# One weight tensor and one transfer per unit of an expert layer, and six scatters instead of eight for its last chunk

## The chip, the cores and the metric

The kernel runs on one core of one Trainium2 chip. The metric is the device time of one execution in microseconds; the median of several runs is taken.

## The reference

The input is a batch of 32 images of 224 x 224. Each image becomes S = 1024 tokens of D = 64 numbers (patches of 7 x 7 times a matrix, plus a bias and a position). Two layers follow:

```
h = tok(x)                                # 32 x 1024 x 64
h = layernorm(h + attention(h))           # one head, softmax over 1024 keys
h = layernorm(h + ffn(h))

ffn: E = 8 experts, 256 hidden, top 1
  expert = argmax(softmax(h @ gate_w + gate_b)), prob = its probability
  the first CAP = 5120 tokens of each expert are kept, others give 0
  y = (relu(row @ w1[e] + b1[e]) @ w2[e] + b2[e]) * prob
```

All of it is in float32. What matters here is the expert layer: each of the 32768 tokens goes through the two matrices of its own expert, and the result goes back to the token's place.

## The kernel before, in words

**Two halves, interleaved.** A window b (the loop in `run_windows`, -2 to 33) works on attention for image b, prepares images b+1 to b+4, and finishes image b-1. Window b also scatters the 1024 rows of image b-2, each with its probability and token number (ROW = 66 numbers), from SBUF to a table in DRAM (`slots`), sorted by expert: GpSimd issues 8 indirect transfers of 128 rows (`scatter`, L1305). From the same table the expert layer reads units: 256 rows in a line (UNIT), all of one expert. Four units are a chunk, and there are NC = 34 chunks. VectorE works out from the counts per expert which units come next (`full_units` to `name_last`) and writes a table `tab` with a place and an expert for each.

**Where chunks run.** Chunks 0 to 26 run inside windows 6 to 32 (HOST), spread between the steps of attention. The remaining seven, 27 to 33, run after the last window, in `rounds`, where nothing else is left but the scatters. The last image's table (its chunks are 29 to 33, LAST = 29) names up to 20 units, for what is then left of every expert; a unit that has no rows is read from a dummy place whose token numbers are FAR, beyond the bounds check, so that its rows are written nowhere.

**One chunk.** SyncE's `load_chunk` (L407 to L431) waits for `table_ready`, reads four entries of `tab` into registers (L412), waits for the scatters of the images concerned and for the buffer to come free (NBUF = 5), and then issues, for each of the four units k with v = k // 2 and u = k % 2, three transfers: the rows to `b_in` (L427), the expert's w1 with b2 as a last column to `b_w1`, in the half of the partitions of u (L428), and its w2 with b1 as last columns to `b_w2`, on all partitions (L430). Each adds 16 to `c_loaded`, so TensorE and ScalarE wait for 96 per pair of units. The four units are two pairs v; in each, unit u = 0 sits on partitions 0 to 63 and u = 1 on 64 to 127 where rows are transposed.

Then: `rows_beside` (ScalarE L789) copies rows to `b_x`; `rows_turn` (TensorE L601) transposes them; `xT_copy` (ScalarE L796); `up` (TensorE L633, twice 4 products with w1); `rectify` (ScalarE L807, relu with b1); `down` (TensorE L649, 8 products with w2 that leave both units of a pair above each other); `sums_copy` (ScalarE L815 and L816) adds b2 and moves the sums to `b_yT`; `turn_back` (TensorE L610) transposes them back; on VectorE `weigh` (L1128), `finite` (L1135, L1136), `to_numbers` (L1141 to L1146), `residual_sum` (L1153 to L1158) and `centre` (L1162, L1166); `squares` (ScalarE L823), `sum_of_squares` (VectorE L1173), `deviation` (ScalarE L829), `scaled` (VectorE L1177, L1179) writes the finished rows `b_o`; and GpSimd's `spread_out` scatters them to the output with 8 indirect transfers of 128 rows (L1317). Tile j of the eight is u * 4 + v * 2 and 0 or 1, so tiles 6 and 7 are the unit k = 3.

**What sets the order.** Each engine has its list written out by hand. In `rounds` TensorE has, per chunk c: up(c, 0), turn_back(c-1), up(c, 1), rows_turn(c+1), down(c). VectorE has sum_of_squares(c-1), weigh(c), finite(c), scaled(c-1), and so on. GpSimd scatters chunks 25 to 33 one after the other after the last image's rows; before the first tile of chunk 29 (LAST) it waits until all scatters of earlier chunks have landed, as two of them may write one row. SyncE loads chunks 27 to 33 one after the other and then waits for the last scatters of each output buffer (L472).

In the windows, `sums_copy` reads the bank `p_misc`, and `qk_product` of a later image (TensorE L503) is the next to write there; it waits for `b_yT_ready`. From L503, `hi` and `lo` are made (ScalarE L744, VectorE L957) and copied by SyncE to `mQ`, `sK`, `mR` and `sR` (L444 to L461).

Of the kernel before, what the change touches and what calls it, by code (L numbers as in the profile page):

```python
# [18 lines left out]
D = 64  # L19
PATCH = 49  # L20
P = 128
# [61 lines left out]

def build(nc, x, posT, wqk, wide, deep, w1, w2, out):
    slots = nc.dram_tensor("slots", (SLOTS, ROW), F32, kind="Internal").ap()
    with ExitStack() as ctx:
# [107 lines left out]

        b_w1 = sb("b_w1", [P, NBUF, PAIRS, W1C])
        b_w2 = sb("b_w2", [P, NBUF, PAIRS, 2, W2C])
        b_in = sb("b_in", [P, NBUF, 2, CT, ROW])
# [188 lines left out]
        def _(sp):  # L386
# [20 lines left out]
            def load_chunk(c):  # L407
# [16 lines left out]
                for k in range(2 * PAIRS):  # L424
                    v, u = k // 2, k % 2
                    t = slice(v * UT, (v + 1) * UT)
                    sp.dma_start(b_in[:, r, u, t, :], unit_rows(at[k])).then_inc(c_loaded[r], 16)  # L427
                    sp.dma_start(b_w1[u * D:(u + 1) * D, r, v, :],  # L428
                                 w1[bass.ds(e[k], 1), :, :].rearrange("a k f -> (a k) f")).then_inc(c_loaded[r], 16)
                    sp.dma_start(b_w2[:, r, v, u, :], w2[bass.ds(e[k], 1), :, :].rearrange("a k f -> (a k) f"))\  # L430
                        .then_inc(c_loaded[r], 16)  # L431
# [39 lines left out]
            for r in range(NOUT):  # L471
                sp.wait_ge(b_scattered[r], 16 * NT * len(range(r, NC, NOUT)))  # L472


        @block.tensor
        def _(pe):
# [112 lines left out]
            def rows_turn(c):  # L589

                r = c % NBUF
                pe.wait_ge(c_loaded[r], 96 * PAIRS * (c // NBUF + 1))
                pe.wait_ge(b_x_ready, c + 1)
# [19 lines left out]
            def up(c, f):  # L613
# [16 lines left out]
                for v in range(PAIRS):  # L630
                    for u in range(2):
                        h = slice(u * D, (u + 1) * D)
                        pe.matmul(place[:, u, v * UNIT:(v + 1) * UNIT], b_w1[h, r, v, f * P:(f + 1) * P],  # L633
                                  b_xT[h, v, :], start=True, stop=True).then_inc(b_h_done, 1)

            def down(c):
# [9 lines left out]
                for v in range(PAIRS):  # L646
                    for f in range(HB):
                        for u in range(2):
                            last = pe.matmul(place[u * D:(u + 1) * D, v * UNIT:(v + 1) * UNIT],  # L649
                                             b_w2[:, r, v, u, f * D:(f + 1) * D], b_h[:, f, u, v, :],  # L650
                                             start=(f == 0), stop=(f == HB - 1))
# [77 lines left out]
        def _(act):  # L729
# [53 lines left out]
            def rows_beside(c):  # L783

                r = c % NBUF
                act.wait_ge(c_loaded[r], 96 * PAIRS * (c // NBUF + 1))
                if c >= 1:
# [11 lines left out]
            def rectify(c, f):  # L799
# [3 lines left out]
                for u in range(2):  # L803

                    act.wait_ge(b_h_done, 2 * PAIRS * (HB * c + f) + 2 * (PAIRS - 1) + u + 1)
                    for v in range(PAIRS):
                        act.activation(b_h[:, f, u, v, :], place[:, u, v * UNIT:(v + 1) * UNIT], ACT.Relu,  # L807
                                       bias=b_w2[:, r, v, u, HB * D + f:HB * D + f + 1]).then_inc(b_relu, 1)

            def sums_copy(c):  # L810
                r = c % NBUF
                act.wait_ge(b_y_done, c + 1)
                if c >= 1:
                    act.wait_ge(b_back_done, c)
                act.activation(b_yT[:, 0, :], banks(c)[2][:, 0:UNIT], ACT.Identity, bias=b_w1[:, r, 0, FF:W1C])  # L815
                act.activation(b_yT[:, 1, :], banks(c)[2][:, UNIT:2 * UNIT], ACT.Identity,  # L816
                               bias=b_w1[:, r, 1, FF:W1C]).then_inc(b_yT_ready, 1)

# [439 lines left out]
        def _(pool):  # L1258
# [89 lines left out]
            def rounds():  # L1348
                for c in range(INSIDE - 2, NC):
                    spread_out(c)  # L1350
            run_windows(step, rounds)

_INS = ["x", "posT", "wqk", "wide", "deep", "w1", "w2"]

# [58 lines left out]
```

## Time and profile before

| | |
|---|---|
| three runs | 1132.54, 1133.03, 1133.87 us |
| median | 1133.03 us |
| the profiled execution | 1133.07 us |
| its span, first to last instruction | 1131.2 us |
| TensorE busy (share of the span) | 1017.4 us (90%) |
| VectorE busy | 895.8 us (79%) |
| ScalarE busy | 690.0 us (61%) |
| GpSimd busy | 694.4 us (61%) |
| SyncE's transfers of weights | 136 of 65.0 KB and 136 of 64.2 KB |
| mean granted clock of TensorE | 0.949 of full speed |

Engines in the rows below: PE is TensorE's products, PEld its weight loads, DVE VectorE, ACT ScalarE, POOL GpSimd, SPq SyncE's queue. In a row of the timeline the first number is the start in microseconds from the span's start, the second the duration; then engine, line, operation, output<-input, partitions x elements, and in brackets the idle time before it and what ended it. TensorE's durations are modelled, and GpSimd's are rough.

### The profile page before, as it was taken

The page shows a single profiled execution, that of the slowest core. Times are in us where ns is not written, and L with a number is a line of the kernel's source. Part 1 is how long each engine was busy: PE and PEld are TensorE (multiplying, and loading weights), DVE is VectorE, ACT ScalarE, POOL GpSimd, SP SyncE. Part 2 cuts the span into 40 slices and gives each one's busy share as a digit, 9 for nine tenths or more (in the row PEclk, how much of TensorE's full clock was granted, in tenths as well). Part 3 has the DMA queues.
Part 4 walks back from the last instruction along what each step waited for, and adds up shares of the span by engine and source line. Part 5 has one row for each costly group of instructions (what it writes and reads, how often), then busy time and mean ns, then how long its engine had stood idle before and what let it go on. Part 6 is the DMA issues. An engine that isn't in the chain of part 4 may idle for free.

```text
span 1131.2 us, 19202 instructions
## 1 busy us (share of the span) xinstructions
PE 1017.4 (90%) x5534; PEld 575.3 (51%) x5534; DVE 895.8 (79%) x1843; ACT 690.0 (61%) x1073; POOL 694.4 (61%) x696
## 2 busy tenths in 40 slices
PE   4899999999999999999999999999999999855630
PEld 2455555555555555555555555555555555433320
DVE  5667787789888888989898988889898979475770
ACT  2355545667777677776667777766776666644530
POOL 0014444446767676666677676766766767777775
PEclk8699999999999999999999999999999999956875
DMA  5424334443435353444434343535344432123300
GB/s 129 100 70 102 97 90 116 102 108 93 117 100 131 87 135 99 118 114 102 103 104 117 92 119 97 135 87 134 99 117 109 99 76 62 34 67 94 100 29 8
DMA packets 87679, 110.01 MB, mean 97 GB/s; under 512 B 18892, under 2 KB 63903, under 8 KB 87574
## 3 DMA queue, kind: packets, MB, share of 16 engines
q1 hardware_dynamic: 70678, 91.67, 34.0%
q0 software_dynamic: 16896, 17.12, 4.7%
q8 instruction: 45, 0.74, 0.3%
q14 instruction: 60, 0.49, 0.1%
HBM read 40.69 MB, written 18.17 MB: 52 GB/s over the span
## 4 chain that ended last, share of the span: by engine, by line
PE 58%; DVE 25%; issue 6%; SPq 4%; POOL 2%; ACT 2%; DMA 2%; POOLq 0%; DVEq 0%; ACTq 0%
PE p_u L570 16%; PE p_st L554 9%; DVE mx L964 9%; PE p_st L557 7%; PE p_sm L540 6%; PE p_misc L503 4%; PE p_misc L526 4%; PE p_misc L585 3%; PE p_misc L633 3%; PE p_misc L649 2%; DVE ld L1015 2%; POOL out L1317 2%; SPq L428 1%; ACT xh L749 1%; SPq L427 1%
## 5 line engine op out<-in xcount | busy, mean ns | idle before, releaser
L1305 POOL DMA_INDIRECT slots<-rows,idx x256 | 261.4, 1021 | 216.7 <-issue 147.3
L964 DVE TENSOR_REDUCE mx<-p_sm 128x1 f32<-128x1024 f32 x252 | 307.3, 1220 | 78.9 <-PE p_sm L540 78.5
L766 ACT ACTIVATE pT<-p_st 128x1024 f32<-128x1024 f32 x256 | 262.2, 1024 | 162.5 <-PE p_st L557 158.9
L1317 POOL DMA_INDIRECT out<-b_o,b_ix x272 | 284.4, 1046 | 95.1 <-issue 73.3
L570 PE MATMUL p_u<-pT,vv 128*64 128x512 f32 x1024 | 262.9, 613 | 0.0
L554 PE MATMUL p_st<-mQ,sK 128*128 128x512 f32 x512 | 183.7, 440 | 5.3 <-ACT pT L766 3.4
L557 PE MATMUL p_st<-mR,sR 72*128 72x512 f32 x512 | 161.8, 397 | 0.0
L540 PE MATMUL p_sm<-sK,mQ 64*128 64x512 f32 x252 | 130.8, 519 | 7.1 <-DVE mx L964 3.4
L554 PEld LDWEIGHTS p_st<-mQ,sK 128*128 128x128 f32 x512 | 79.5, 189 | 103.6 <-issue 85.4
L540 PE MATMUL p_sm<-hi,mQ 64*128 64x512 f32 x252 | 130.6, 518 | 0.0
L557 PEld LDWEIGHTS p_st<-mR,sR 72*128 72x128 f32 x512 | 97.2, 190 | 22.6
L570 PEld LDWEIGHTS p_u<-pT,vv 128*64 128x64 f32 x1024 | 56.5, 135 | 96.2 <-issue 78.7
L807 ACT ACTIVATE b_h<-p_misc,b_w 128x256 f32<-128x256 f32 x244 | 95.5, 474 | 8.5 <-PE p_misc L633 3.9
L744 ACT ACTIVATE hi<-p_misc 128x1024 fp32r<-128x1024 f32 x32 | 32.8, 1024 | 100.7 <-PE p_misc L503 100.7
L540 PEld LDWEIGHTS p_sm<-sK,mQ 64*128 64x128 f32 x252 | 46.9, 186 | 87.4 <-issue 57.1
L1278 POOL TENSOR_TENSOR uc<-tt,hh 128x576 f32<-128x576 f32 x32 | 42.1, 1316 | 73.1 <-DVE tt L991 72.1
L526 PE MATMUL p_misc<-w_px,xt 114*128 114x137 f32 x504 | 76.6, 296 | 0.0
L633 PE MATMUL p_misc<-b_xT,b_w 64*128 64x256 f32 x488 | 73.3, 421 | 3.3 <-ACT b_h L807 1.7
L526 PEld LDWEIGHTS p_misc<-w_px,xt 114*128 114x128 f32 x504 | 63.7, 192 | 15.4 <-issue 15.4
L585 PEld LDWEIGHTS p_misc<-w_j,uu 128*128 128x128 f32 x512 | 62.0, 192 | 5.0 <-ACT uu L771 2.4
L585 PE MATMUL p_misc<-w_j,uu 128*128 128x73 f32 x512 | 61.1, 272 | 1.1 <-ACT uu L771 1.1
L633 PEld LDWEIGHTS p_misc<-b_xT,b_w 64*128 64x128 f32 x488 | 44.6, 197 | 30.3 <-issue 22.8
(191 smaller groups left out, 1508.0 us busy)
## 6 DMA issues: line engine op xcount, KB each, us to landing
mQ<-hi SPq DMA_DIRECT2D x64, 256.0 KB, 3.9
b_in<-slots SPq DMA_DIRECT2D x136, 66.0 KB
b_w<-in_w SPq DMA_DIRECT2D x136, 65.0 KB
b_w<-in_w SPq DMA_DIRECT2D x136, 64.2 KB
sK<-hi SPq DMA_DIRECT2D x32, 256.0 KB, 4.6
sK<-lo SPq DMA_DIRECT2D x32, 256.0 KB, 5.3
mR<-lo SPq DMA_DIRECT2D x32, 256.0 KB, 4.2
sR<-hi SPq DMA_DIRECT2D x32, 256.0 KB, 5.1
```

The source lines that it names most:

```text
L526: last = pe.matmul(projected(n, r)[:, j // 2, (j % 2) * GP:(j % 2 + 1) * GP], xt[0:KTOK, p, t * P:(t + 1) * P], w_px[:, :], start=True, st ...
L540: last = pe.matmul(max_place(n, j)[:, a, :], mQ[t][h, j * P:(j + 1) * P], keys[h, a * HALF:(a + 1) * HALF], start=True, stop=True)
L554: pe.matmul(p_st[:, a, :], sK[t][:, k * P:(k + 1) * P], mQ[t][:, a * HALF:(a + 1) * HALF], start=True, stop=False)
L557: last = pe.matmul(p_st[:, a, :], sR[p][0:D + NT, k * P:(k + 1) * P], mR[p][0:D + NT, a * HALF:(a + 1) * HALF], start=False, stop=True)
L570: last = pe.matmul(p_u[c:c + D, a, :], vv[:, p, k, :], pT[k % 4][:, a * HALF:(a + 1) * HALF], start=(r == 0), stop=(r == 3))
L585: last = pe.matmul(p_misc[:, j // 4, (j % 4) * GT:(j % 4 + 1) * GT], uu[:, j * P:(j + 1) * P], w_j[:, :], start=True, stop=True)
L633: pe.matmul(place[:, u, v * UNIT:(v + 1) * UNIT], b_w1[h, r, v, f * P:(f + 1) * P], b_xT[h, v, :], start=True, stop=True).then_inc(b_h_don ...
L766: act.activation(pT[k % 4][:, :], flat(p_st), ACT.Exp).then_inc(exp_done, 1)
L807: act.activation(b_h[:, f, u, v, :], place[:, u, v * UNIT:(v + 1) * UNIT], ACT.Relu, bias=b_w2[:, r, v, u, HB * D + f:HB * D + f + 1]).the ...
L964: dve.tensor_reduce(mx[:, p, j:j + 1], flat(max_place(n, j)), AX.X, ALU.max).then_inc(max_done, 1)
L1305: pool.indirect_dma_start(slots, bass.IndirectOffsetOnAxis(ap=idx[:, p, j:j + 1], axis=0), rows[:, p, j, :], None, bounds_check=SLOTS - 1, ...
L1317: pool.indirect_dma_start(out_rows, bass.IndirectOffsetOnAxis(ap=b_ix[:, o, j:j + 1], axis=0), b_o[:, o, j, :], None, bounds_check=T - 1, ...
```

## The change

On the host, w1 (with b2 as its column) is stored twice, one copy under the other, so that it has 128 rows, and beside it, in the same tensor, w2 and b1: `w` has 8 x 128 x 387 numbers. A unit's weights come in one transfer on all 128 partitions to `b_w`, at [v, u], so w1 lies on both halves of the partitions for either unit, and a half is read. A load has 8 transfers instead of 12 and the waits count 64 instead of 96. Since the column of b2 now lies at another place for u = 0 than for u = 1, `sums_copy` has four operations on 64 partitions and 256 columns instead of two on 128 partitions. For the last chunk `spread_out` leaves out tiles 6 and 7, and SyncE's last wait expects 32 less for its buffer.

```diff
--- before.py
+++ after.py
@@ -81,7 +81,7 @@
 DEEP = (KTOK, D, D, D, E, 1, KA)
 
 
-def build(nc, x, posT, wqk, wide, deep, w1, w2, out):
+def build(nc, x, posT, wqk, wide, deep, w, out):
     slots = nc.dram_tensor("slots", (SLOTS, ROW), F32, kind="Internal").ap()
     with ExitStack() as ctx:
         def sb(name, shape, dt=F32):
@@ -192,8 +192,7 @@
         t_rc = sb("t_rc", [P, LEFT])
         tab = sb("tab", [P, UNITS], U32)
 
-        b_w1 = sb("b_w1", [P, NBUF, PAIRS, W1C])
-        b_w2 = sb("b_w2", [P, NBUF, PAIRS, 2, W2C])
+        b_w = sb("b_w", [P, NBUF, PAIRS, 2, W1C + W2C])
         b_in = sb("b_in", [P, NBUF, 2, CT, ROW])
         b_x = sb("b_x", [P, CT, 2 * D])
         b_xT = sb("b_xT", [P, PAIRS, UNIT])
@@ -425,9 +424,8 @@
                     v, u = k // 2, k % 2
                     t = slice(v * UT, (v + 1) * UT)
                     sp.dma_start(b_in[:, r, u, t, :], unit_rows(at[k])).then_inc(c_loaded[r], 16)
-                    sp.dma_start(b_w1[u * D:(u + 1) * D, r, v, :],
-                                 w1[bass.ds(e[k], 1), :, :].rearrange("a k f -> (a k) f")).then_inc(c_loaded[r], 16)
-                    sp.dma_start(b_w2[:, r, v, u, :], w2[bass.ds(e[k], 1), :, :].rearrange("a k f -> (a k) f"))\
+
+                    sp.dma_start(b_w[:, r, v, u, :], w[bass.ds(e[k], 1), :, :].rearrange("a k f -> (a k) f"))\
                         .then_inc(c_loaded[r], 16)
 
             def step(b, c, third, has):
@@ -469,7 +467,8 @@
 
 
             for r in range(NOUT):
-                sp.wait_ge(b_scattered[r], 16 * NT * len(range(r, NC, NOUT)))
+                missing = 16 * UT if r == (NC - 1) % NOUT else 0
+                sp.wait_ge(b_scattered[r], 16 * NT * len(range(r, NC, NOUT)) - missing)
 
 
         @block.tensor
@@ -589,7 +588,7 @@
             def rows_turn(c):
 
                 r = c % NBUF
-                pe.wait_ge(c_loaded[r], 96 * PAIRS * (c // NBUF + 1))
+                pe.wait_ge(c_loaded[r], 64 * PAIRS * (c // NBUF + 1))
                 pe.wait_ge(b_x_ready, c + 1)
                 if c < INSIDE:
                     pe.wait_ge(t_ready, min(HOST[c], NB))
@@ -630,7 +629,7 @@
                 for v in range(PAIRS):
                     for u in range(2):
                         h = slice(u * D, (u + 1) * D)
-                        pe.matmul(place[:, u, v * UNIT:(v + 1) * UNIT], b_w1[h, r, v, f * P:(f + 1) * P],
+                        pe.matmul(place[:, u, v * UNIT:(v + 1) * UNIT], b_w[h, r, v, u, f * P:(f + 1) * P],
                                   b_xT[h, v, :], start=True, stop=True).then_inc(b_h_done, 1)
 
             def down(c):
@@ -647,7 +646,7 @@
                     for f in range(HB):
                         for u in range(2):
                             last = pe.matmul(place[u * D:(u + 1) * D, v * UNIT:(v + 1) * UNIT],
-                                             b_w2[:, r, v, u, f * D:(f + 1) * D], b_h[:, f, u, v, :],
+                                             b_w[:, r, v, u, W1C + f * D:W1C + (f + 1) * D], b_h[:, f, u, v, :],
                                              start=(f == 0), stop=(f == HB - 1))
                 last.then_inc(b_y_done, 1)
 
@@ -783,7 +782,7 @@
             def rows_beside(c):
 
                 r = c % NBUF
-                act.wait_ge(c_loaded[r], 96 * PAIRS * (c // NBUF + 1))
+                act.wait_ge(c_loaded[r], 64 * PAIRS * (c // NBUF + 1))
                 if c >= 1:
                     act.wait_ge(b_t_done, c)
                 act.activation(b_x[:, :, :].rearrange("p j (u d) -> p u j d", d=D), b_in[:, r, :, :, 0:D], ACT.Copy)\
@@ -805,16 +804,19 @@
                     act.wait_ge(b_h_done, 2 * PAIRS * (HB * c + f) + 2 * (PAIRS - 1) + u + 1)
                     for v in range(PAIRS):
                         act.activation(b_h[:, f, u, v, :], place[:, u, v * UNIT:(v + 1) * UNIT], ACT.Relu,
-                                       bias=b_w2[:, r, v, u, HB * D + f:HB * D + f + 1]).then_inc(b_relu, 1)
+                                       bias=b_w[:, r, v, u, W1C + HB * D + f:W1C + HB * D + f + 1]).then_inc(b_relu, 1)
 
             def sums_copy(c):
                 r = c % NBUF
                 act.wait_ge(b_y_done, c + 1)
                 if c >= 1:
                     act.wait_ge(b_back_done, c)
-                act.activation(b_yT[:, 0, :], banks(c)[2][:, 0:UNIT], ACT.Identity, bias=b_w1[:, r, 0, FF:W1C])
-                act.activation(b_yT[:, 1, :], banks(c)[2][:, UNIT:2 * UNIT], ACT.Identity,
-                               bias=b_w1[:, r, 1, FF:W1C]).then_inc(b_yT_ready, 1)
+                for v in range(PAIRS):
+                    for u in range(2):
+                        h = slice(u * D, (u + 1) * D)
+                        last = act.activation(b_yT[h, v, :], banks(c)[2][h, v * UNIT:(v + 1) * UNIT], ACT.Identity,
+                                              bias=b_w[h, r, v, u, FF:W1C])
+                last.then_inc(b_yT_ready, 1)
 
             def squares(c):
                 act.wait_ge(b_c_ready, c + 1)
@@ -1346,14 +1348,17 @@
                     scatter(b - 2, par, range(6, NT))
 
             def rounds():
-                for c in range(INSIDE - 2, NC):
+                for c in range(INSIDE - 2, NC - 1):
                     spread_out(c)
+
+
+                spread_out(NC - 1, range(NT - UT))
             run_windows(step, rounds)
 
 
 
 
-_INS = ["x", "posT", "wqk", "wide", "deep", "w1", "w2"]
+_INS = ["x", "posT", "wqk", "wide", "deep", "w"]
 
 
 def kernel(x, L0_tok_W, L0_tok_b, L0_tok_pos, L0_attn_Wq, L0_attn_bq, L0_attn_Wk, L0_attn_bk, L0_attn_Wv,
@@ -1387,8 +1392,7 @@
         "posT": columns(np.asarray(L0_tok_pos)[0].T),
         "wqk": np.concatenate([np.concatenate([wq.T, wk.T], axis=1),
                                np.concatenate([np.asarray(L0_attn_bq), np.asarray(L0_attn_bk)])[None]]),
-        "w1": up,
-        "w2": np.concatenate([down, bias1], axis=2),
+        "w": np.concatenate([np.concatenate([up, up], axis=1), down, bias1], axis=2),
         "wide": np.concatenate([
             np.eye(P, dtype=f), np.triu(np.ones((P, P), f), 1), sumcol,
             np.broadcast_to(np.arange(E, 0, -1, dtype=f), (P, E)),
```

## Rows read from the trace of the kernel before

**Rows 1.** The page: span, and the shares of the chain that ended last, by engine

```profile
span 1131.2 us, 19202 instructions
...
PE 58%; DVE 25%; issue 6%; SPq 4%; POOL 2%; ACT 2%; DMA 2%; POOLq 0%; DVEq 0%; ACTq 0%
```

**Rows 2.** Two windows; columns: stretch, length, busy PE, PEld, DVE, ACT, POOL, clock, DMA

```profile
861.90:923.20 61.30, 60.84 (x343) 34.56 (x344) 53.12 (x111) 42.28 (x65) 41.86 (x43) 1.00 0.42 103
```

**Rows 3.** The chain that ended last, from 990 us on, by line

```profile
by line: issue 24.0%; POOL out L1317 11.5%; SPq L428 10.0%; SPq L427 8.1%; SPq L430 7.8%; SPq L412 5.0%; POOL slots L1305 3.9%; DMA slots<-rows,idx 3.1%; DMA b_w<-in_w 2.7%; PE p_sm L649 2.6%; DVE b_o L1179 1.5%; DVE b_p L1128 1.5%; PE p_mi
```

**Rows 4.** SyncE's queue, load of chunk 29 and start of chunk 30's: start us, us

```profile
1026.90 0.34 SPq L427 DMA_DIRECT2D b_in<-slots  x1
1027.47 0.50 SPq L428 DMA_DIRECT2D b_w<-in_w  x1
1028.16 0.43 SPq L430 DMA_DIRECT2D b_w<-in_w  x1
1028.84 0.33 SPq L427 DMA_DIRECT2D b_in<-slots  x1
...
1033.87 0.45 SPq L430 DMA_DIRECT2D b_w<-in_w  x1
1036.92 0.34 SPq L427 DMA_DIRECT2D b_in<-slots  x1
```

**Rows 5.** The scatters of chunks 25 to 33: ns min/median/max, first and last start us

```profile
L1317 POOL DMA_INDIRECT out<-b_o,b_ix x72: 970/972/1490, 1025.7 to 1122.8; - x72
```

**Rows 6.** GpSimd in order of time: start, us, idle before it in brackets

```profile
1045.44 1.12 POOL L1317 DMA_INDIRECT out<-b_o,b_ix  x1 [0.30 <-issue]
1047.35 1.11 POOL L1317 DMA_INDIRECT out<-b_o,b_ix  x1 [0.79 <-DVE b_o L1179]
...
1068.09 1.49 POOL L1317 DMA_INDIRECT out<-b_o,b_ix  x1 [0.30 <-issue]
1071.85 0.97 POOL L1317 DMA_INDIRECT out<-b_o,b_ix  x1 [2.28 <-issue]
...
1113.84 0.97 POOL L1317 DMA_INDIRECT out<-b_o,b_ix  x1 [0.30 <-issue]
...
1122.77 0.97 POOL L1317 DMA_INDIRECT out<-b_o,b_ix  x1 [0.30 <-issue]
```

**Rows 7.** VectorE in order of time: b_o of chunks 27 and 33, one b_fin between

```profile
1045.86 0.69 DVE L1179 TENSOR_TENSOR b_o<-b_c,b_rs 128x512 f32<-128x512 f32 x1
...
1053.06 0.43 DVE L1135 TENSOR_SCALAR b_fin<-b_p 128x512 uint8<-128x512 f32 x1
...
1101.79 0.69 DVE L1179 TENSOR_TENSOR b_o<-b_c,b_rs 128x512 f32<-128x512 f32 x1
```

**Rows 8.** The end: GpSimd's drain and SyncE past its last wait (ns, start us)

```profile
L86 POOLq DRAIN  x1: 22557/22557/22557, 1108.5 to 1108.5; - x1
L86 SPq COMPARE_BRANCH  x1: 41/41/41, 1124.9 to 1124.9; - x1
```

**Rows 9.** Landing: one kind of issue (us from issue), one piece of the chain (start, us)

```profile
mQ<-hi SPq DMA_DIRECT2D x64, 256.0 KB, 3.9
...
1075.55 1.87 DMA b_w<-in_w
```

**Rows 10.** ScalarE waits for chunk 29's load

```profile
1035.88 0.63 ACT L789 ACTIVATE b_x<-b_in 128x512 f32<-128x512 f32 x1 [5.31 <-DMA b_w<-in_w]
```

**Rows 11.** A window, ScalarE and TensorE around the copy of the sums

```profile
802.53 0.47 ACT L815 ACTIVATE b_yT<-p_misc,b_w 128x256 f32<-128x256 f32 x1 [0.72 <-PE p_misc L649]
...
802.90 0.47 ACT L816 ACTIVATE b_yT<-p_misc,b_w 128x256 f32<-128x256 f32 x1
...
805.13 0.71 PE L503 MATMUL p_misc<-xh,w_qkh 114*128 114x512 f32 x2
```

**Rows 12.** ScalarE on 128 and on 50 partitions

```profile
806.81 1.02 ACT L744 ACTIVATE hi<-p_misc 128x1024 fp32r<-128x1024 f32 x1 [2.93 <-PE p_misc L503]
...
810.68 1.05 ACT L749 ACTIVATE xh<-xr 50x1024 fp32r<-50x1024 f32 x1
```

## The prediction

> **What bounds the kernel now.** The profiled execution took 1133.07 us, 1131.2 of it span and 1.87 around it; the median of the three runs, 1133.03, is 0.04 below it, so the sum is made against 1133.07 and moved by 0.04. I read the page first: the chain that ended last is TensorE for 58% and VectorE for 25% of the span, and SyncE's queue for only 4% [rows 1]. The reader is to ask where those 4% lie, since 136 of SyncE's transfers go away.
>
> Next, the windows view. In two windows of 61.3 us TensorE is busy for 60.84 and VectorE for 53.12, with the DMA engines at 0.42 [rows 2]. So in the windows, up to about 988 us, compute sets the time.
>
> Then the chain from 990 us on: SyncE's L427, L428, L430 and L412 stand in it with 31% together [rows 3]; of 142 us these are 44, or 3.9% of the span, so all of SyncE's 4% lie here and none in the windows. The timeline of its queue shows why. One unit costs 1.94 us of queue (1026.90 to 1028.84) and a chunk 10.02 (1026.90 to 1036.92), of which L428 takes 1028.16 - 1027.47 = 0.69 us per unit [rows 4]. A reader who stops here takes the rounds for bound by loads.
>
> GpSimd's view says otherwise. The 72 scatters of chunks 25 to 33 start between 1025.7 and 1122.8 us, median 0.97 us each [rows 5], and the last eight stand (1122.77 - 1113.84) / 7 = 1.276 us apart [rows 6]. 71 such steps are 90.6 us of the 97.1. The rest: 0.79 us of idle time instead of 0.30 before chunk 27, 2.28 instead of 0.30 before chunk 29 (the wait at LAST for all scatters before it), together 2.47, and about 4.0 by which scatters beside VectorE's work are longer than 0.97, up to 1.49 [rows 6]. Chunk 33's rows were ready at 1101.79 + 0.69 = 1102.48 [rows 7], yet its first scatter starts at 1113.84 [rows 6]: GpSimd is 11.4 us behind. It is the bound of the rounds, at 8 x 1.276 = 10.2 us a chunk, and SyncE's 10 us a chunk are hidden behind it. After the last scatter (1122.77 + 0.97 = 1123.74) SyncE passes its last wait at 1124.9, and GpSimd's drain, begun at 1108.5 us for 22.56, ends at 1131.06 [rows 8].
>
> **The change, part by part.**
>
> Two scatters go. They are the last to start on a saturated engine, nothing lies beside them, and nothing hides them: 2 x 1.276 = **-2.55 us**. The drain ended 7.3 us after the last scatter; I let it follow one for one. If it didn't follow at all, the end would stay; it is bounded by 0 and 2.55, and I take 2.55, since the drain is GpSimd's own. SyncE's final wait asks for 32 less on the semaphore of chunk 33, which are just these two.
>
> Four issues per chunk go, 136 in all. In the rounds a chunk's load gets 4 x 0.69 = 2.76 us shorter on the queue. Where does this matter for GpSimd? Only at its one wait for rows, before chunk 27: b_o of chunk 27 ended at 1045.86 + 0.69 = 1046.55 us [rows 7], and its scatter started 0.80 later [rows 6]. That b_o stands on VectorE behind weigh of chunk 28, which goes back to sums_copy and down of chunk 28, which stand on TensorE behind rows_turn of chunk 29, which waits for chunk 29's load. The load can't begin earlier (it waits for the last image's scatters, on GpSimd); its last issue would stand at 1033.87 - 2.76 = 1031.11. What is not shown is how long 198 KB take to land. The old b_w piece of 66 KB took 1.87 us, the 256 KB of mQ 3.9 [rows 9]; between them by size, 3.2, with 1.9 and 3.9 as ends. Now ScalarE starts on that chunk at 1035.88, 2.0 after the issue [rows 10]; then at 1031.11 + 3.2 = 34.3, 1.5 us earlier (0.9 to 2.9). The copy of the sums, below, gives back 0.74. Left are 0.8 us (0.1 to 2.1), and the wait is worth 0.79 - 0.30 = **-0.49 us** (0.1 to 0.49). From there on, GpSimd is the slower one again in each round, and the shorter loads are worth nothing.
>
> In the windows, the 2.76 us per window are worth nothing: SyncE is in no part of the chain there [rows 1, 3], and TensorE is busy all through [rows 2]. What stands behind the load in its queue (the patches, mR and sR) goes out 2.7 us earlier, and nobody waits for it. If TensorE's cover were gone, this would be a gain, not a cost.
>
> More bytes: w1 is loaded for both halves, 66 KB per unit more, 264 KB per window. At 0.42 of DMA share and 103 GB/s [rows 2] that is 264 KB in 30.65 us, 9 GB/s more, and the share goes to some 0.46. Cost 0, under TensorE's 60.84 of 61.3 us. In the rounds a unit brings 266 KB in 1.25 us of queue; if transfers were slower than that, they would still hide behind the 10.2 us of scatters. Bounds: -0.5 and +1.0 over the whole kernel.
>
> sums_copy becomes four operations of 64 partitions instead of two of 128. The two start 0.37 us apart and last 0.47 [rows 11]. For half the partitions no row shows the same operation; nearest is a copy of 1024 columns, 1.02 us on 128 partitions and 1.05 on 50 [rows 12], so I take 0.37 for each added one: +0.74 us per chunk, with 0 and 4 x 0.47 - 0.84 = 1.04 as ends. In a window the next to want p_misc is TensorE's qk_product: b_yT was ready at 802.90 + 0.47 = 803.37, and L503 started at 805.13 [rows 11], 1.76 us of slack, so nothing shows. In the rounds 0.74 lies on the way to b_o, counted above. For chunk 33 it delays b_o from 1102.48 against a need at 1113.84: nothing.
>
> VectorE against GpSimd: scatters beside VectorE's work take up to 1.49 us, those with none beside them 0.97 [rows 6], 4.0 us in all. VectorE's operations stay the same in number, and all still stand beside scatters, so I leave the 4.0 as it is (3.5 to 4.5). Here a rule bears. The Trainium skill (SBUF — State Buffer, "SBUF: two separate sides") has the port pair of VectorE and GpSimd as an exclusive lock, under which GpSimd can't write descriptors until the VectorE operation ends. The trace agrees that there is a cost, but 0.52 us at most is less than one whole b_o of 0.69. That rule as a full block is a rival below.
>
> Sum: 1133.07 - 2.55 - 0.49 = 1130.03, less the 0.04 to the median: **1130.0 us**, 0.27% faster.
>
> **The rivals.**
>
> The rounds are bound by loads (0.05). For it: the chain's 31%. The five loads from chunk 29 to 33 would each give 2.76, less 1.3 for the later landing at the end: -12.5, and with -2.55 and -0.04 this is 1118.0 us. Against it: 0.30 us of idle time before nearly each scatter, and the 11.4 us of backlog.
>
> The end doesn't follow, or the windows pay a little (0.23, both land at no change). If the drain gives back less than one for one, 1130.5 to 1132.5. If each of the 27 windows with a chunk pays 0.05 to 0.1 us for the added copies and bytes, +1.4 to +2.7: 1131.4 to 1132.7. For it: nothing but that TensorE has under 0.5 us of slack in 61.3 [rows 2]. Against it: 1.76 us of slack at the hand-over.
>
> VectorE shuts GpSimd out for longer (0.04, slower). Place: the rounds, where shorter loads draw VectorE's operations closer together. If b_fin, b_pos and b_neg (0.43 each) and b_o (0.69) [rows 7] each held a scatter back for their full length, seven rounds would cost 7 x 1.98 = 13.9 instead of 4.0: +9.9, and with the 3.0 of gain 1139.9 us. It decides once the stretching grows by 5.3 us (3.0 of gain and 2.3 of the 0.2%), from 0.57 to 1.3 us a round. Against it: the rounds already take 10 us with VectorE's seven inside, and never did. The Trainium skill's SBUF page, named above, states this full block, and by it the result would be this rival's.
>
> **How the numbers follow.** About 0.2%, 2.3 us, is what a measurement of this kernel can tell from no change. The forecast has 0.68; the load rival 0.05 is faster too, and the case of no change 0.23, slower 0.04. The forecast's own range, from its bounds: -0.1 on the second term to -0.49, ±1 for bytes and stretching, ±0.5 for the runs' spread: 1129.0 to 1131.4. To hold 8 in 10 I go up to 1131.9, into the second case, and leave out the load rival and the slower one. Of the forecast's 0.68 a part (0.02) falls above 1130.77, so faster 0.71, same 0.25, slower 0.04.
>
> **What would show it.** 70 scatters instead of 72 in the last stretch, still 1.276 apart at the end, with chunk 27's first after 0.30 of idle time and not 0.79; the last scatter's end about 1120.7; the drain's end 7.3 us behind it; SyncE's chunk in the rounds 7.3 us instead of 10.0 and the wait of rows_turn shorter, yet the backlog before chunk 33 grown beyond 11.4; windows still 61.3 us a pair; L503 not waiting for the copies. I am wrong if the pairs lengthen by 0.1 or more, if the 2.28 us before chunk 29 change, or if GpSimd waits for b_o in the later rounds.

## The result, and the profile after

The kernel after took 1129.37 us (median of 22 runs, 1126.3 to 1132.0) where the kernel before, run on the same chip in turns with it, took 1131.65 (22 runs). The ratio is 0.997, with an interval of 0.9961 to 0.9979: 3.4 us faster, 2.4 to 4.4; the two medians lie 2.28 us apart. The prediction was 3.04 us and 1130.0. The profiled execution took 1127.63 us, 5.4 less than the profiled one before. The predicted gain is thus near the measured one in these runs, below it in the second series further down (5.0 us, 3.4 to 6.6) and too small in the pair of traces, so the question is where these 5.4 us lie, and which of them belong to the change.

The page of after: span, chain by engine, and SyncE's queue q1 (packets, MB, share of the 16 engines).

```profile
span 1125.8 us, 18858 instructions
q1 hardware_dynamic: 59798, 100.61, 35.8%
PE 59%; DVE 25%; issue 7%; ACT 4%; POOL 3%; DMA 1%; SPq 1%; POOLq 0%; DVEq 0%; ACTq 0%
b_w<-in_w SPq DMA_DIRECT2D x136, 193.5 KB
```

SyncE's queue had 4% of the chain [rows 1] and now has 1%. That is some 34 us of the chain, and the kernel is not 34 us faster: the chain only runs another way through the rounds. From 990 us on, by line:

```profile
by line: issue 25.0%; PE p_sm L648 14.8%; POOL out L1319 12.2%; ACT b_h L806 11.0%; ACT b_yT L817 6.1%; POOL slots L1307 6.0%; ACT b_sq L825 2.8%; DVE b_vs L1175 2.6%; DMA b_w<-in_w 2.2%; DMA slots<-rows,idx 1.6%; ACT b_x L788 1.5%; SPq L42
```

Where SyncE's lines stood with 31% [rows 3], there are now TensorE's `down` (L648), ScalarE's `rectify` (L806) and the copies of the sums (L817). A chain follows one of several paths of nearly the same length; the share of a path is not what shortening it brings.

The stretch from the first window's product of `qk_product` to the one near 897 us holds most of the windows; then the window of [rows 2] (columns as there).

```profile
63.05:896.53 833.48, 827.21 (x4557) 466.74 (x4556) 715.09 (x1445) 583.62 (x883) 526.97 (x523) 1.00 0.45 114
861.90:923.20 61.30, 60.75 (x344) 34.53 (x342) 53.08 (x110) 44.46 (x71) 41.77 (x42) 1.00 0.43 110
```

And the same stretch before:

```profile
64.40:897.48 833.08, 826.97 (x4558) 466.62 (x4556) 715.33 (x1445) 558.45 (x837) 527.06 (x523) 1.00 0.43 106
```

ScalarE has 25.2 us more to do, and the DMA engines carry 114 GB/s instead of 106; the length goes from 833.08 to 833.48. SyncE's load of chunk 29 and the start of chunk 30's, as in [rows 4]:

```profile
1025.70 0.33 SPq L426 DMA_DIRECT2D b_in<-slots  x1
1026.25 0.33 SPq L428 DMA_DIRECT2D b_w<-in_w  x1
1026.84 0.33 SPq L426 DMA_DIRECT2D b_in<-slots  x1
...
1030.02 0.34 SPq L428 DMA_DIRECT2D b_w<-in_w  x1
...
1032.97 0.34 SPq L426 DMA_DIRECT2D b_in<-slots  x1
```

A unit costs 1.14 us (1.94 before), a chunk 7.27 (10.02). GpSimd in the rounds, all 70 scatters and then in order of time, as in [rows 5, 6]:

```profile
L1319 POOL DMA_INDIRECT out<-b_o,b_ix x70: 969/972/1488, 1024.5 to 1117.5; - x70
```

```profile
1046.00 1.05 POOL L1319 DMA_INDIRECT out<-b_o,b_ix  x1 [0.30 <-issue]
...
1065.64 1.20 POOL L1319 DMA_INDIRECT out<-b_o,b_ix  x1 [0.30 <-issue]
1068.85 0.97 POOL L1319 DMA_INDIRECT out<-b_o,b_ix  x1 [2.01 <-issue]
...
1111.12 0.97 POOL L1319 DMA_INDIRECT out<-b_o,b_ix  x1 [0.30 <-issue]
...
1117.50 0.97 POOL L1319 DMA_INDIRECT out<-b_o,b_ix  x1 [0.30 <-issue]
```

Chunk 27's first scatter (1046.00) no longer waits for its rows. The last ends at 1118.47, and the drain 7.1 us later (1106.8 + 18.74 = 1125.54), to be read beside [rows 8]:

```profile
L86 POOLq DRAIN  x1: 18743/18743/18743, 1106.8 to 1106.8; - x1
L86 SPq COMPARE_BRANCH  x1: 41/41/41, 1119.7 to 1119.7; - x1
```

Cut at four marks, the 5.40 us of span are these. "Stretching" is the sum over the scatters of what each took beyond 0.972 us.

| stage | before | after | difference |
|---|---|---|---|
| start to the product of the first window | 64.40 | 63.05 | -1.35 |
| from it to the product near 897 us | 833.08 | 833.48 | +0.40 |
| from there to chunk 25's first scatter | 128.23 | 127.97 | -0.26 |
| that scatter to the end of the last | 98.03 | 93.97 | -4.06 |
| of it: two scatters, 2 x 1.276 | | | -2.55 |
| of it: wait before chunk 27 | 0.79 | 0.30 | -0.49 |
| of it: wait before chunk 29 | 2.28 | 2.01 | -0.27 |
| of it: stretching | 3.90 | 3.12 | -0.78 |
| last scatter to the end | 7.46 | 7.33 | -0.13 |

### The profile page after: what moved, and what is told of

Its sections match the earlier page's. It is cut to its first block, busy times and chain, and to the rows that moved or that the text cites. A ratio compares the mean times of both kernels' runs of the same rounds, so it can differ in the third digit from the quotient of the medians.

```text
span 1125.8 us, 18858 instructions
## 1 busy us (share of the span) xinstructions
PE 1019.9 (91%) x5534; PEld 576.2 (51%) x5534; DVE 895.2 (80%) x1843; ACT 727.6 (65%) x1141; POOL 691.4 (61%) x694
## 3 DMA queue, kind: packets, MB, share of 16 engines
q1 hardware_dynamic: 59798, 100.61, 35.8%
## 4 chain that ended last, share of the span: by engine, by line
PE 59%; DVE 25%; issue 7%; ACT 4%; POOL 3%; DMA 1%; SPq 1%; POOLq 0%; DVEq 0%; ACTq 0%
PE p_u L569 16%; PE p_st L553 9%; DVE mx L966 9%; PE p_st L556 7%; PE p_sm L539 6%; PE p_misc L502 4%; PE p_misc L525 4%; PE p_misc L584 3%; PE p_misc L632 3%; PE p_misc L648 2%; PE p_sm L648 2%; POOL out L1319 2%; DVE ld L1017 2%; ACT b_h L806 1%; ACT xh L748 1%
## 5 line engine op out<-in xcount | busy, mean ns | idle before, releaser
L806 ACT ACTIVATE b_h<-p_misc,b_w 128x256 f32<-128x256 f32 x244 | 95.6, 475 | 8.2 <-PE p_misc L632 3.4
L525 PEld LDWEIGHTS p_misc<-w_px,xt 114*128 114x128 f32 x504 | 63.7, 192 | 15.5 <-issue 15.5
## 6 DMA issues: line engine op xcount, KB each, us to landing
b_w<-in_w SPq DMA_DIRECT2D x136, 193.5 KB
```

Source lines behind the costliest of these rows:

```text
L525: last = pe.matmul(projected(n, r)[:, j // 2, (j % 2) * GP:(j % 2 + 1) * GP], xt[0:KTOK, p, t * P:(t + 1) * P], w_px[:, :], start=True, st ...
```

## The experiments

Two figures are read from each profiled execution: the **rest**, the span less the start-up up to that first product (1066.80 us before, 1062.75 after), and the **tail**, from chunk 25's first scatter to the end of the last (98.03 and 93.97).

The diffs show the lines that make the experiment; the waits that count the same transfers or scatters were changed with them and are left out.

**What is the kernel's, and what the execution's?** The kernel after once more, unchanged (no diff).

> The kernel after, not altered: a second execution to see what is the kernel's and what is the execution's. Theory: from the first window's product near 64 us to the end it takes 1062.75 us again, within 0.3; what lies before that product, which no part of the change touches, comes out anywhere between 62.5 and 67 us. Rival (the 63.05 us of the first execution is of the change's making): 63.05 again, within 0.3, and the span 1125.8.

Measured: ratio 0.9956 [0.9942, 0.997], that is 5.0 us, where the first series gave 3.4. The product stands at 65.29 us, not at 63.05, the span is 1127.3, the rest 1062.01 and the tail 93.79.

```profile
65.29:898.22 832.93, 826.83 (x4557) 467.20 (x4556) 716.20 (x1445) 583.42 (x883) 526.71 (x523) 1.00 0.45 114
```

In eleven profiled executions of ten kernels that product lies anywhere from 62.56 to 67.12 us, and no edit touches what runs ahead of it. So the -1.35 is not the change's. The rest differs by 0.74 between two executions of one kernel, more than the 0.3 I had allowed, and most of that is the long stretch (833.48, 832.93); before (833.08) lies between them, so the +0.40 is no cost that can be shown. The tail repeats within 0.2, and it is the stage to compare.

**The two parts apart.** The kernel before with the scatters' edit alone, and the kernel after without it:

```diff
-                for c in range(INSIDE - 2, NC):
+                for c in range(INSIDE - 2, NC - 1):
                     spread_out(c)
+                spread_out(NC - 1, range(NT - UT))
```

> Theory A (GpSimd's 80 steps of 1.276 us set the end of the rounds): two scatters fewer alone give -2.55 us, the end follows one for one, GpSimd's drain ends 7.3 us after the last scatter. Idle time before chunk 27 (0.79 us) and before chunk 29 (2.28 us) stays. Rival B (the rounds are bound by SyncE's loads): 0 us. Rival C (the windows pay for the weights' part of the change): the windows here are those of before, and this version beats the whole change by what they pay.

> Theory A: the one wait before chunk 27 goes (-0.49 us), the wait at chunk 29 and the stretched scatters give some tenths (-1.0 us in the trace of the whole change), the windows pay up to +0.4 us: -0.5 to -1.5 us. Rival B (loads bound the rounds): -12 us. Rival C (the windows pay): 0 or slower.

Measured, scatters alone: ratio 0.9972 [0.9961, 0.9984], rest 1064.21 (-2.59), tail 95.65 (-2.38). Weights alone: 0.9982 [0.9968, 0.9995], rest 1065.24 (-1.56), tail 96.53 (-1.50). The two rests add up to -4.15, and both edits together gave -4.05. The weights' edit thus gives a little more than the 0.5 to 1.5 us expected of it. GpSimd before chunk 29, with the scatters' edit alone and with the weights' alone:

```profile
1070.00 1.49 POOL L1318 DMA_INDIRECT out<-b_o,b_ix  x1 [0.31 <-issue]
1074.01 0.97 POOL L1318 DMA_INDIRECT out<-b_o,b_ix  x1 [2.52 <-issue]
```

```profile
1064.94 1.21 POOL L1318 DMA_INDIRECT out<-b_o,b_ix  x1 [0.30 <-issue]
1068.17 0.97 POOL L1318 DMA_INDIRECT out<-b_o,b_ix  x1 [2.02 <-issue]
```

The wait at LAST goes with the scatter ahead of it. Where that scatter was stretched to 1.49 us the wait was 2.28 [rows 6] or 2.52; where it took 0.97 to 1.21, in eight other executions, it was 2.01 or 2.02 (in the eleventh, weights_in_four, GpSimd waits there for b_o). The 0.27 so comes from which scatter VectorE meets, and appears with the weights' edit. That edit also brings the stretching down: 2.84 us alone, against 3.90 before and 4.04 with the scatters' edit.

The wait before chunk 27 did not do what was expected of it. With the scatters' edit alone it is 0.56 us (0.79 was to stay), and with the weights' edit alone it is 0.60 and not gone:

```profile
1044.58 1.23 POOL L1318 DMA_INDIRECT out<-b_o,b_ix  x1 [0.60 <-issue]
```

Here b_o of chunk 27 ends 19.98 us after chunk 25's first scatter and the scatter starts at 20.77, 0.79 later, as before (20.84 and 21.64). GpSimd came to the wait earlier, because fewer of the scatters ahead of it were stretched. Wait and stretching ahead of it are one term: as long as b_o comes last, what one loses the other gains.

**The issues or the copies?** The kernel after, with w1's own half and w2 in transfers of their own again, so that a chunk has twelve issues and only the copies of the sums differ from before:

```diff
-                    sp.dma_start(b_w[:, r, v, u, :], w[bass.ds(e[k], 1), :, :]...
+                    sp.dma_start(b_w[h, r, v, u, 0:W1C], w[bass.ds(e[k], 1), h, 0:W1C]...
+                    sp.dma_start(b_w[:, r, v, u, W1C:W1C + W2C], w[bass.ds(e[k], 1), :, W1C:W1C + W2C]...
```

> The whole change, but w1 for its own half alone and w2 in a transfer of their own again: 12 issues per chunk and the bytes of before, with the four operations for the sums and the six scatters. Theory A: the shorter loads are worth at most 1.5 us of the whole change, so -1.5 to -2.6 us against before, with chunk 27 waiting again, by 1 us more than before, since the sums come 1.06 us later. Rival B: no gain beside before. If the windows' +0.4 us come from the bytes they are gone here; if from the four operations, they stay.

Measured: ratio 0.9984 [0.9972, 0.9996], tail 95.59, that is 1.62 over after.

```profile
1049.98 1.11 POOL L1323 DMA_INDIRECT out<-b_o,b_ix  x1 [2.21 <-DVE b_o L1185]
```

Chunk 27's first scatter waits 2.21 us, 1.91 more than after. Its b_o of chunk 27 ends at 21.80 us from chunk 25's first scatter, 1.88 later than after and 0.96 later than before. So at this one place the added copies cost about what they last, and the four issues taken away pay for them with room to spare; everywhere else twelve issues bring no wait. With twelve issues stretching (2.82) and the wait at LAST (2.02) are as low as after. The number of issues is not their cause. What this version shares with after and not with scatters_only is the four copies; that these move the rhythm of ScalarE and VectorE in the useful direction is argued from that, not tested by itself. Its long stretch takes 832.72 us, so neither bytes nor issues show there.

**How far are the loads from being the bound?** The kernel after, with the weights of chunks 27 to 33 in four transfers of 32 partitions:

```diff
+PARTS = [1 if c < INSIDE else 4 for c in range(NC)]
-                    sp.dma_start(b_w[:, r, v, u, :], w[bass.ds(e[k], 1), :, :]...
+                    for g in (slice(i * P // PARTS[c], (i + 1) * P // PARTS[c]) for i in range(PARTS[c])):
+                        sp.dma_start(b_w[g, r, v, u, :], w[bass.ds(e[k], 1), g, :]...
```

> The kernel after, with the weights of a unit in four transfers of 32 partitions for chunks 27 to 33, the bytes the same: 20 issues a chunk in place of 8. By undisturbed steps of 0.57 us an issue a chunk's load takes 11.4 us and some 2.5 between chunks, 14 in all, over the 10.3 to 11.0 us in which GpSimd issues a chunk's scatters. Theory (GpSimd bounds the rounds only as long as SyncE's load is shorter than it): chunk 33's load ends near 1096 instead of 1074, its rows follow some 23 us later and its last scatter 8 us after those, so the kernel ends 5 to 15 us later than after, 1134 to 1144. Rival (the loads are far enough ahead that the rounds still end by GpSimd's count): 1128 to 1131.

Measured: 1145.01 us, ratio to before 1.0113 [1.0086, 1.0139]; tail 109.49, 15.5 over after. SyncE, ScalarE and GpSimd, a row or two of each:

```profile
1054.67 0.36 SPq L429 DMA_DIRECT2D b_in<-slots  x1
...
1068.53 0.36 SPq L429 DMA_DIRECT2D b_in<-slots  x1
```

```profile
1053.46 0.63 ACT L792 ACTIVATE b_x<-b_in 128x512 f32<-128x512 f32 x1 [2.60 <-DMA b_w<-in_w]
```

```profile
1052.05 1.11 POOL L1323 DMA_INDIRECT out<-b_o,b_ix  x1 [1.88 <-DVE b_o L1185]
```

Now a load does last longer (13.9 us between these two starts) than a chunk of scatters, GpSimd waits for b_o ahead of each chunk from 26 to 31, and the tail follows: seven waits make 17.8 us, 14.0 more of idle time than after has, and stretching is 4.67 (+1.55). This is how a round bound by loads looks, and neither before nor after looks like it. The tail is half a microsecond beyond the 15 us that I had allowed, and the median about one beyond 1144. I had reckoned from chunk 33's load to its own rows; but TensorE turns the rows of chunk c + 1 ahead of `down` of chunk c, and VectorE makes b_o of chunk c - 1 behind `weigh` of c, so the load of chunk 33 holds back the rows of chunk 31, and three chunks of scatters follow it.

**Does the end follow?** The kernel after without any scatter of chunk 33 (its rows are not written):

```diff
-                spread_out(NC - 1, range(NT - UT))
```

> The whole change without the other six scatters of the last chunk (its rows are left out). Theory A: 6 x 1.276 = 7.66 us less than the whole change, about -11 us against before (0.990), the drain's end 7.3 us behind the last scatter; the backlog is then chunk 32's. Rival (the end doesn't follow GpSimd one for one, a floor by the drain): less than 6 us beyond the whole change.

Measured: ratio 0.9887 [0.987, 0.9904]; rest 1054.54, tail 85.89. Against the two executions of after the tail is 8.08 and 7.90 shorter; six steps of 1.276 are 7.66, the rest is stretching. The end comes 6.86 us behind the last scatter (7.33 after): it follows one for one and a little more.

**How much room has the hand-over of the sums?** In the windows of after the four copies last 1.90 us, and the next product in their bank starts 1.24 us behind their end (835.12 - 833.88), in the other kind of window 0.69 (804.03 - 803.34). Before it was 1.76 in that one [rows 11].

```profile
801.43 1.91 ACT L817 ACTIVATE b_yT<-p_misc,b_w 64x256 f32<-64x256 f32 x4 [0.72 <-PE p_misc L648]
...
804.03 0.71 PE L502 MATMUL p_misc<-xh,w_qkh 114*128 114x512 f32 x2
...
831.98 1.90 ACT L817 ACTIVATE b_yT<-p_misc,b_w 64x256 f32<-64x256 f32 x4
...
835.12 0.71 PE L502 MATMUL p_misc<-xh,w_qkh 114*128 114x512 f32 x2
```

To see whether that slack is the room there is, the copies of the windows are cut into eight operations of 128 columns, and into sixteen of 64:

```diff
+                        for part in (range(4) if c < INSIDE else (slice(0, UNIT),)):
+                            n = slice(part * D, part * D + D) if c < INSIDE else part
-                        last = act.activation(b_yT[h, v, :], ...
+                            last = act.activation(b_yT[h, v, n], ...
```

> The whole change with sums_copy in eight operations of 64 partitions x 128 columns in the windows (chunks 0 to 26), four in the rounds. Theory A (the hand-over of p_misc has slack, 0.69 us in one kind of window and 1.24 in the other, with the copies at 1.90 us): eight operations last about 8 x 0.37 = 3.0 us, so 1.1 us more, which shows as 0.4 us in 12 of 23 windows and not in the others: +5 us against the whole change, with TensorE's qk_product waiting for the sums there. Rival (ScalarE has more slack than the rows show, the chain takes another way): no change against the whole change. Rival (the slack was already gone with four): +1.1 us in each of 23 windows, +25 us.

Measured: ratio 0.9974 [0.9959, 0.9988], rest 1063.44, nothing to tell from after, where 5 us more were expected. I had the eight too long: they last 2.50 us and end 0.15 us before the product.

```profile
803.80 2.50 ACT L820 ACTIVATE b_yT<-p_misc,b_w 64x128 f32<-64x128 f32 x8 [0.72 <-PE p_misc L648]
...
806.45 0.70 PE L502 MATMUL p_misc<-xh,w_qkh 114*128 114x512 f32 x2
```

> The kernel after, with the sums of a window's chunk copied by sixteen operations of 64 x 64 instead of four of 64 x 256. Theory (the copies have a slack of their own at the hand-over to the image's products, 0.69 us in one kind of window and 1.24 in the other, and eight operations of 2.50 us in all used up all but 0.14 and 0.65 of it): the sixteen last about 4.0 us, 1.5 longer than the eight, so the hand-over is late by about 1.3 us in one kind and 0.9 in the other, and 22 windows are 15 to 30 us longer; the whole about 1145 to 1160. Rival (another releaser of the same operations hides it, so that the slack that I read is not the room there is): 1127 to 1133, as with eight.

Measured: 1148.6 us, ratio 1.0142 [1.0115, 1.017]; rest 1082.78, 19.3 over the eight.

```profile
788.99 3.67 ACT L820 ACTIVATE b_yT<-p_misc,b_w 64x64 f32<-64x64 f32 x16
...
792.80 0.71 PE L502 MATMUL p_misc<-xh,w_qkh 114*128 114x512 f32 x2 [0.69 <-ACT b_yT L820]
```

Now TensorE does wait for the copies: 23 times before L502, 18.3 us in all, where it did so in no window after. The sixteen are 1.17 us longer than the eight; less what those left over (0.15 and 0.65) that is 1.02 and 0.52 a window, some 18 us over 23 windows. So the slack read in the trace is the whole cover, with nothing else behind it, and the change spent 1.07 of its 1.76 us without a price.

**What stretches the scatters?** The kernel after without `finite` and `to_numbers` in chunks 27 to 33, that is without the replacing of numbers that are not finite: five VectorE operations a round less (the test for finite numbers, two clamps, their sum and the copy by the test). `residual_sum` reads b_p in place of b_n.

```diff
-                    finite(c)
+                    if c < INSIDE:
+                        finite(c)
-                    to_numbers(c)
+                    if c < INSIDE:
+                        to_numbers(c)
```

> The whole change without the replacement of numbers that are not finite in chunks 27 to 33 (b_fin, b_pos, b_neg, b_n are left out and b_p is added as it is): five of VectorE's operations less per round. Theory A (GpSimd bounds the rounds, VectorE touches the end only by stretching scatters beside it, 3.2 us in all): -1 to -2.5 us against the whole change, by shorter scatters and not by earlier rows. Rival (the stretching doesn't come from VectorE): 0. Rival (VectorE bounds the rounds): 7 x 2.5 = -17 us.

Measured: ratio 0.9977 [0.9966, 0.9988], rest 1060.78, tail 91.90. Stretching falls from 3.12 to 0.76 us, and the scatters longer than 1.0 us from 17 to 4.

```profile
L1327 POOL DMA_INDIRECT out<-b_o,b_ix x70: 969/972/1264, 1028.7 to 1119.6; - x70
```

The tail is 2.07 us shorter (stretching -2.36, a wait of 0.56 before chunk 28 +0.26). What VectorE does beside them is what lengthens the scatters. The ratio does not show these 2 us (it is no lower than after's), and this profiled execution had the longest start-up of all, 67.12 us.

The traces show how. Scatters of before [rows 6] and after, and VectorE beside them:

```profile
1068.03 0.73 DVE L1146 COPY_PREDICATED b_n<-b_fin,b_p 128x512 f32<-128x512 uint8 x1
```

```profile
1065.30 0.69 DVE L1181 TENSOR_TENSOR b_o<-b_c,b_rs 128x512 f32<-128x512 f32 x1
```

```profile
1044.73 0.97 POOL L1319 DMA_INDIRECT out<-b_o,b_ix  x1 [0.30 <-DVE b_o L1181]
1044.79 0.69 DVE L1146 TENSOR_TENSOR b_n<-b_pos,b_neg 128x512 f32<-128x512 f32 x1
```

The copy ran when the scatter of 1068.09 started, and ended at 1068.76; the scatter ended at 1069.58, 0.82 later. b_o ended at 1065.99; the scatter that had started within it, at 1065.64, ended at 1066.84, 0.85 later. b_n, which began after its scatter, cost that scatter nothing. In the rounds of the eleven executions 172 of 768 scatters started when an operation of these kinds or a TENSOR_SCALAR had begun over 0.03 us before and had over 0.13 us to run, and each ended 0.80 to 0.85 us after the operation did. Where the operation in progress was a TENSOR_REDUCE or b_p, which reads PSUM (142 scatters), 140 took 0.97, and of the other 454, with none or one just begun or nearly over, 453 took 0.97 or 0.98. So a scatter's stretching is what is left of one operation at the scatter's start, less the first 0.13 us.

## Where the prediction was right, and the step that failed

**The bound.** Right: GpSimd bounds the rounds, and SyncE's 10 us a chunk were hidden. The rival with loads as the bound asked for -12.5; the weights' edit alone gave -1.56, and of the loads tried only the one of 13.9 us a chunk shows loads as the bound.

**Two scatters, -2.55.** Right. Alone they gave -2.59 in the rest and -2.38 in the tail, and the end followed.

**Shorter loads, -0.49 before chunk 27.** Right in place and working, and in the size of the wait; its worth was counted too high. 193.5 KB landed 3.01 us after the last issue (3.2 taken): ScalarE starts at 1033.05, the issue at 1030.02. Counted from chunk 25's first scatter, b_o of chunk 27 ended at 19.92 us instead of 20.84, 0.9 earlier where 0.8 was predicted, and the wait went to 0.30. But chunk 27's first scatter itself started only 0.14 us earlier (21.50 instead of 21.64), since more of the scatters ahead of it were stretched; in the second execution of after it was 0.75 earlier (20.89), and with the weights' edit alone 0.60 us of wait stayed. The term should have been taken together with the stretching ahead of it.

```profile
1030.02 3.01 DMA b_w<-in_w
```

```profile
1033.05 0.63 ACT L788 ACTIVATE b_x<-b_in 128x512 f32<-128x512 f32 x1 [5.82 <-DMA b_w<-in_w]
```

**The copies, +0.74 in length and 0 in price.** The price was right, the length not: four copies of 64 partitions last 1.90 us, +1.06, just beyond my upper end of 1.04. Two on 128 partitions started 0.37 apart [rows 11]; the four start 0.48 apart, each after the end of the one before. Had the cover been under 1.06 instead of 1.76, the error would have cost 0.3 us in each of 23 windows for every 0.3 missing; that is an estimate from sums_in_sixteen, where 23 windows paid.

**More bytes, 0.** Right: the long stretch is 832.93 and 833.48 against 833.08, with q1 at 100.61 MB.

**The backlog before chunk 33, to grow beyond 11.4 us.** Wrong, without a price. It fell to 7.5:

```profile
1102.90 0.69 DVE L1181 TENSOR_TENSOR b_o<-b_c,b_rs 128x512 f32<-128x512 f32 x1
```

b_o of chunk 33 ends at 1103.59 and its first scatter starts at 1111.12. Counted from chunk 25's first scatter its rows are ready at 79.09 us (76.77 before; 78.90 in the second execution, 79.10 with the weights' edit alone), so with shorter loads they come later and not earlier. Two things lie on their way: 1.06 us more of copies in each round, and TensorE's clock, granted at 0.80 between 1025 and 1100 us before and at 0.73 after, both means of time at 2.4 and at 1.2 GHz (columns as in [rows 2]; before, then after):

```profile
1025.00:1100.00 75.00, 41.27 (x252) 24.27 (x248) 49.08 (x98) 34.93 (x87) 56.10 (x55) 0.80 0.29 76
```

```profile
1025.00:1100.00 75.00, 41.54 (x228) 23.34 (x224) 47.55 (x96) 40.41 (x95) 56.54 (x56) 0.73 0.34 94
```

No run tells the two apart. GpSimd is still behind by 7.5 us, which is why nothing was lost.

**VectorE and the scatters, 4.0 unchanged.** This step failed. After has 3.12 and 2.94 us, below my lower end of 3.5, and the wait at LAST, which I had put at no change without a reason though I named it among the signs of being wrong, gives 0.27 more. The two together are -1.05, and they make up the difference between the tail predicted (-3.04) and the one measured (-4.06). I had argued that as many operations stand beside scatters as before; but a scatter pays only for what is left of the operation in progress at its start, that is decided by tenths of a microsecond, and the whole rhythm had moved by nearly one. Over the ten executions that keep VectorE's operations the sum lies anywhere from 1.95 (sums_in_sixteen) to 4.67 us (weights_in_four). That it fell and did not rise was luck: no step of the change's working makes it smaller.

**The Trainium skill's rule** (SBUF — State Buffer, "SBUF: two separate sides"). The page has an exclusive lock between GpSimd and a VectorE operation in a two-port mode, or with two SBUF inputs if GpSimd's operation reads SBUF too: the one that starts first has the port pair for its whole instruction. The 172 scatters agree with it as far as GpSimd waits: each is held until the VectorE operation ahead of it ends, and neither TENSOR_REDUCE nor b_p holds one (the profile does not show an operation's mode). I had read both the rule and the trace wrongly. That 0.52 us, the longest stretching, is less than the 0.69 of a b_o says nothing against a full block, since the operation was already under way. And the rival's price, each operation at its full length, 13.9 us, is not what the rule makes of these rounds: from the operations in progress at the scatters' starts (end + 0.84 us) the sum is 3.27 us after and 4.14 before, and 3.12 and 3.90 were measured. The rival's +9.9 is out. The other half of the rule, VectorE held for a whole scatter, does not show: b_o and b_n took their 0.69 us inside a scatter, while b_fin, when it began 0.52 to 0.63 us into one, took 0.70 and 0.59 instead of 0.43.

**The number.** Against the first series the prediction is 0.4 us short of the middle of an interval of 2.4 to 4.4 us, and against the second 2.0 short (3.4 to 6.6). Against the one profiled execution it is 2.4 short: 1.0 of it the tail, 1.35 the start-up, and this second part no argument from the change could have given.

## What to carry to other kernels

A path's share of the chain is not its worth: ask for the engine that has a backlog, since only its own work and its own waits move the end. Before an operation on a covered path is lengthened, read the gap between its end and its reader's start; that gap was here the whole of the cover, down to 0.15 us. When a change shifts the rhythm of two engines that disturb each other, look in the timeline at what one was doing when the other started, give the disturbance a range from zero up and do not carry its sum over unchanged; do not add a wait and the stretching ahead of it as if they were independent; and take an expected gain of a few microseconds from the stage where it arises, because the start-up alone moved by 4.6 us between executions.

## What was not expected of the hardware

ScalarE's operations on 64 partitions did not overlap at all where those on 128 did by 0.10 us, and cutting them in columns is cheap: 4, 8 and 16 operations took 1.90, 2.50 and 3.68 us. I have no run that tells why the first differ.

Behind a scatter stretched to 1.49 us the wait for its landing was longer as well, 2.28 and 2.52 us from its end instead of 2.01, in the two executions that had one there. Why stays open.

In weights_in_four, where b_o releases each chunk's first scatter, the first three take 1.11, 1.26 and 1.35 us in five of six rounds: b_o is followed by the same operations each time, so each scatter meets the same remainder of one, and the stretching repeats to a hundredth.

What moves the start-up by up to 4.6 us stays open. TensorE's granted clock between 20 and 40 us was 0.56 before (a mean of a little time at 2.4 GHz and more at 1.2) and 1.00, all of it 2.4 GHz, in the second execution of after (columns as in [rows 2]):

```profile
20.00:40.00 20.00, 12.12 (x37) 7.08 (x38) 13.21 (x12) 3.46 (x6) 0.00 (x0) 0.56 0.71 176
```

```profile
20.00:40.00 20.00, 13.62 (x37) 8.10 (x38) 12.95 (x11) 3.45 (x6) 0.00 (x0) 1.00 0.70 172
```

Their first products stood at 64.40 and 65.29 us, so the lower clock there does not go with the later product. TensorE had under 14 of the 20 us to do in both.
